# A third layer with three pair buffers, and VectorE's order there by pairs of tiles

## What is computed

```
h = relu(layernorm(x)); x = x + L0(h, adj)    # attention with adj as mask, both signs, elu
h = relu(layernorm(x)); x = x + L1(h, adj)    # relu((D^-1/2 adj D^-1/2 h) W + b)
h = relu(layernorm(x)); x = x + L2(h, adj)    # relu(adj (step(h) sign(W)^T))
h = relu(layernorm(x)); x = x + L3(h, adj)    # (1 - t) h W + t adj (h W)
```

## Time and profile before

| | |
|---|---|
| median of 3 runs | 964.89 us (964.3 to 965.39) |
| the profiled execution | 965.67 us, span of its records 964.0 us |
| PE busy | 933.9 us, 97% of the span |
| DVE, ACT, POOL busy | 743.3, 540.9 and 94.1 us |
| third layer | about 698 to 779 us from the span's start |
| fourth layer | about 779 to 964 us |

### The profile page before, as it was taken

The page is one execution under the profiler, slowest core; times in us unless marked ns, Lnnn a source line. Parts: engine busy times, 40 slices in busy tenths (PEclk is TensorE's granted clock), DMA queues, the critical chain, the costliest instruction groups (busy, mean ns, idle before and its releaser), DMA issues.

```text
span 964.0 us, 18964 instructions
## 1 busy us (share of the span) xinstructions
PE 933.9 (97%) x7105; PEld 689.2 (71%) x7105; DVE 743.3 (77%) x1112; ACT 540.9 (56%) x934; POOL 94.1 (10%) x206
## 2 busy tenths in 40 slices
PE   9889999999999999999999999999999989999995
PEld 8457788888888888888888455555788845555553
DVE  7697899999999999999996776656447755655664
ACT  6476899999999999999985611111223331111010
POOL 4100001000010001000030000000024430000000
PEclk9899999999999999999999999999999999999998
DMA  4915276677576666658312425655247726666642
GB/s 178 96 45 77 23 100 76 66 89 96 48 96 83 81 66 86 86 51 109 46 39 100 173 94 203 211 183 203 114 181 281 276 79 213 215 227 205 201 153 65
DMA packets 39883, 120.80 MB, mean 125 GB/s; under 512 B 4604, under 2 KB 24597, under 8 KB 39701
## 3 DMA queue, kind: packets, MB, share of 16 engines
q1 hardware_dynamic: 27653, 97.94, 29.0%
q0 software_dynamic: 10944, 21.30, 25.5%
q10 hardware_dynamic: 1232, 0.85, 0.3%
HBM read 169.48 MB, written 14.50 MB: 191 GB/s over the span
## 4 chain that ended last, share of the span: by engine, by line
PE 84%; DVE 7%; ACT 3%; issue 2%; POOL 2%; DMA 0%; POOLq 0%; DVEq 0%; ACTq 0%
PE f_ya L1318 23%; PE f_yb L1318 23%; PE f_ya L1495 14%; PE f_ya L1433 12%; DVE f_gb L1856 2%; PE f_ya L1269 2%; PE f_yb L1404 2%; PE f_yb L1376 2%; PE f_yb L1269 1%; PE f_ya L1442 1%; POOL f_gv L960 1%; ACT f_ubuf L1184 1%; ACT f_x_mat L1186 1%; DVE f_stats L1600 1%; PE f_yb L1302 1%
## 5 line engine op out<-in xcount | busy, mean ns | idle before, releaser
L1318 PE MATMUL f_ya<-f_x_mat,f_s_mat 128*128 128x257 f16 x2028 | 334.6, 273 | 1.9 <-DVE f_x_mat L1664 1.9
L1318 PE MATMUL f_yb<-f_x_mat,f_s_mat 128*128 128x257 f16 x2028 | 333.2, 273 | 0.0
L1318 PEld LDWEIGHTS f_yb<-f_x_mat,f_s_mat 128*128 128x128 f16 x2028 | 198.2, 98 | 24.8
L1318 PEld LDWEIGHTS f_ya<-f_x_mat,f_s_mat 128*128 128x128 f16 x2028 | 194.5, 98 | 27.2 <-issue 2.8
L1030 ACT ACTIVATE f_gb<-f_e_tile,f_expc 128x256 f32<-128x256 f32 x338 | 144.5, 494 | 9.3 <-DVE f_s_mat L1694 9.3
L1856 DVE SCALAR_TENSOR_TENSOR f_gb<-f_gb 128x1664 f32<-128x1664 f32 x52 | 97.7, 1886 | 18.0 <-DMA f_gb<-adj_dram 18.0
L1689 DVE SCALAR_TENSOR_TENSOR f_s_mat<-f_wm,f_s_mat 128x1792 f16<-128x1792 f32 (+1 forms) x52 | 98.4, 1892 | 12.1 <-ACT f_s_mat L1041 8.5
L1683 DVE TENSOR_TENSOR f_wm<-f_gb,f_a 128x1792 f32<-128x1792 f32 (+1 forms) x52 | 98.1, 1887 | 3.2 <-issue 1.6
L1684 DVE SCALAR_TENSOR_TENSOR f_gb<-f_gb,f_a 128x1792 f32<-128x1792 f32 (+1 forms) x52 | 98.1, 1887 | 0.0
L1694 DVE SCALAR_TENSOR_TENSOR f_s_mat<-f_gb,f_s_mat 128x1792 f16<-128x1792 f32 (+1 forms) x52 | 98.0, 1886 | 0.0
L1041 ACT ACTIVATE f_s_mat<-f_wm 128x1792 f16<-128x1792 f32 (+1 forms) x52 | 82.5, 1587 | 22.0 <-DVE f_wm L1683 20.9
(11 more groups left out here) (185 smaller groups left out, 938.2 us busy)
## 6 DMA issues: line engine op xcount, KB each, us to landing
f_gb<-adj_dram SPq DMA_DIRECT2D x52, 832.0 KB, 5.0
f_a<-f_a_dram SPq DMA_DIRECT2D x23, 832.0 KB, 5.9
f_wm<-f_a_dram SPq DMA_DIRECT2D x16, 832.0 KB, 4.6
f_rows<-adj_dram POOLq DMA_DIRECT2D x24, 416.0 KB, 8.2
f_a<-adj_t_dram POOLq DMA_DIRECT2D x26, 224.0 KB, 4.9
f_a_dram<-f_a SPq DMA_DIRECT2D x26, 224.0 KB, 5.3
f_a<-adj_t_dram POOLq DMA_DIRECT2D x26, 192.0 KB, 6.9
f_a_dram<-f_a SPq DMA_DIRECT2D x26, 192.0 KB, 4.2
```

Of the source, the lines that this page charges most:

```text
L1318: return pe.matmul(bank[:, 0:F + 1], s_mat[:, j, side, i], x_mat[:, j, x_side, 0:F + 1], start=start, stop=stop)
```

## The change

Two things change, both in the third layer.

The first is the buffers and loads. Pairs 3 to 12 go through a ring of three buffers (`wide[0][:, 0]`, `a8[:, 0]`, `a8[:, 1]`) in place of two, and after pair q is done, pair q + 3 is loaded, where it was pair q + 2. Slot 0 of the fourth layer is loaded after pair 2 (before: after pair 2 too), slots 3, 2 and 1 after pairs 10, 11 and 12 (before: slot 1 after pair 3, slots 2 and 3 after pairs 11 and 12). PE's hardware loop over pairs 5 to 12 becomes straight code.

The second is VectorE's order. A pair is now `update(2q)`, `update(2q + 1)`, then the check for pairs 1 to 10, then `norm(2q)`, `norm(2q + 1)`.

```diff
+        def ring2():
+            return [(wide[0][:, 0], extra_here[0], 3), (a8[:, 0], pair_here[2, 0], 1), (a8[:, 1], pair_here[2, 1], 2)]
...
                     if q == 1:
                         load_pair(2, 4, 0)
                         load_pair(2, 5, 1)
-                    elif q < 4:
-                        load_slot(q - 2)
-                    elif q < PAIRS - 2:
-                        load_pair(2, q + 2, q % 2)
+                    elif q == 2:
+                        load_slot(0)
+                    elif q < PAIRS - 3 and q % 3 == 0:
+                        load_extra(q + 3, 0)
+                    elif q < PAIRS - 3:
+                        load_pair(2, q + 3, q % 3 - 1)
                     else:
-                        load_slot(q - PAIRS + 4)
+                        load_slot(PAIRS - q)
...
                 pair2(2, 0, 16, wide[0][:, 1], extra_here[1])
-                pair2(3, 1, 16, wide[0][:, 0], extra_here[0])
-                pair2(4, 0, 32, a8[:, 0], pair_here[2, 0])
-                with pe.Fori(0, (PAIRS - 5) // 2) as k:
-                    for i in range(2):
-                        pair2(2 * k + 5 + i, 1 - i, 16 * k + 32 + 16 * i, a8[:, 1 - i], pair_here[2, 1 - i])
+                for q in range(3, PAIRS):
+                    rows, here, loads = ring2()[q % 3]
+                    pair2(q, q % 2, 16 * ((q - loads) // 3 + 1), rows, here)
...
                             if layer == 2:
                                 update(t, p, k, r=r)
-                                if not (first and p == 0):
-                                    norm(t - 1, 1 - p)
+                                if p == 1 and 0 < k <= CHECKS1 + 4 - CHECKS2:
+                                    check(CHECKS2 + k - 1, (CHECKS2 + k - 1) % 2)
+                                if p == 1:
+                                    norm(t - 1, 0)
+                                    norm(t, 1)
                                 continue
...
                         for q in range(1, PAIRS):
                             pair(q, False, r=q % 2)
-                            if CHECKS2 + q - 1 < CHECKS1 + 4:
-                                check(CHECKS2 + q - 1, (CHECKS2 + q - 1) % 2)
...
-                    if layer == 2:
-                        norm(TILES - 1, 1)
```

## The result

The changed kernel takes 981.24 us (median of 5 runs, 981.03 to 981.36). The kernel before, run beside it, took 964.3 us (5 runs, 961.8 to 965.39). The ratio of the runs is 1.0185 with a 95% interval of 1.0167 to 1.0202 (that of the two medians is 1.0176): **1.9% slower**. The profiled execution took 981.03 us with a span of 979.2 us. In the new file the same statements stand a few lines lower: L963 of before is L969, L956 is L962, L960 is L966, the check L1856 is L1860, the update L1893 is L1897, the low half L1916 is L1920, and PE's L1483 and L1495 are L1489 and L1499.

A forecast was written before the change was run, and what follows sets the result against it. PE was taken as the bound, except in the third layer's loop through VectorE, GpSimd and ScalarE. 710.73 + 6.23 + 10 x 7.62 + 6.23 + 4.15 = 803.54 against 787.20, so 964.89 + 16.3 = 981.2 us; range 972 to 988.5.

The forecast's parts named there:

- the sum: VectorE's new third-layer order: two pairs of 6.23 us and ten of 7.62 move tile 24's low half by +16.3 us.
- The loads, nothing: Third-layer loads through three buffers, and the fourth layer's slots: off the chain, hidden, worth nothing either way.
- A pair without a check, 6.23 us: Third layer, pairs 0 and 11: next update waits behind both tiles' GpSimd and ScalarE rounds, 6.23 us a pair.
- A pair with a check, 7.62 us: Third layer, pairs 1 to 10: check delays GpSimd's L963, VectorE waits 1.2 us per low half, period 7.62 us.
- The cause, the check holding GpSimd up: Third layer: the check's two SBUF inputs hold GpSimd's L963 until 0.09 us after the check, at U+4.43.
- Low half of tile 24 at 803.54 us: End of the third layer: tile 24's low half moves from 787.20 to 803.54 us, +16.3 us.
- The clock at no cost: PE's granted clock: third-layer idling of 1.9 us in 7.6 costs nothing; border gap grows to about 4.3 us.
- up to 1.6 us: Border of third and fourth layers: possible clock cost if the slow stretch after PE's gap doubles.
- PE's gaps put down to L1893: Changed profile, third layer: PE gaps of about 1.9 us attributed to the update L1893, none to a load.
- The other half of the rule: GpSimd's power, begun before the check, holds the check off: some 0.15 us a pair, 982.7 us in all; not used.
- Rival 3: Third layer: VectorE no longer waits, PE bounds at 5.67 us a pair; -5.0 us, 959.9 us; chance 0.04.
- Rival 2: Third layer: check holds GpSimd's power (L960) as well, period 8.33 us; +23.4 us, 988.3 us; chance 0.05.

The follow-up runs named there:

- run 1: Changed kernel's new buffers, loads and straight PE loop, but VectorE's order of before: 964.9 us against 964.88 for the kernel before, ratio 0.9998.
- run 2: Kernel before with only VectorE's new order, keeping its two buffers and loads: 981.73 us, ratio 1.0184 to the kernel before.
- run 3: Changed kernel without the third layer's ten checks, a one-column memset signalling in place of each: 966.95 us, ratio 1.003 to the kernel before.
- run 4: Changed kernel with the third layer's ten checks reading their second input from PSUM instead of SBUF: 964.92 us, ratio 1.0009 to the kernel before.
- run 5: Changed kernel with each of the ten checks cut into two instructions of 832 columns: 979.7 us, ratio 1.0162 to the kernel before.
- run 6: Kernel before plus the three-buffer ring, each low half two tiles after its update, small tensors four deep: 954.22 us, ratio 0.9896.
- run 7: Kernel before with its two buffers and loads, each low half two tiles after its update, small tensors four deep: 954.44 us, ratio 0.9895.
- run 8: Changed kernel with its order by pairs, but the low halves are those of the pair before, small tensors four deep: 954.13 us, ratio 0.9893.

## Why the prediction was right

The mechanism was the one that the sum used, and runs 1 to 8 bear it out step by step. That 981.2 us met 981.24 so closely is luck: the sum was added to a median of three runs, and the runs of before beside the changed kernel lie between 961.8 and 965.39 us.

- **The loads, nothing:** right, shown by runs 1 and 2. No gap of PE is put down to a load any more, VectorE's period stayed at 6.32 us, and the stretch is 77.1 us against 77.0.
- **A pair without a check, 6.23 us:** 716.73 - 710.49 = 6.24 us between the first two updates. Without checks, a pair in the middle takes 6.15 (run 3).
- **A pair with a check, 7.62 us:** 7.65. L963's counterpart ends 0.07 us after the check (0.09 predicted), the two waits of VectorE are 1.18 and 1.20 us (1.2 each). The 0.03 us that are missing come from the check's start, 0.15 us after the last statistics instead of the 0.10 I took from an update, less the 0.02 by which L969 ends sooner.
- **The cause, the check holding GpSimd up:** run 4 shows it by taking away one SBUF input and nothing else on VectorE's timeline. That without the checks about 6.2 us a pair are left, set by two rounds in a row, is shown by run 3 (6.15 us), and that what exceeds PE's 5.68 us is a wait in VectorE's queue by runs 6 to 8.
- **Low half of tile 24 at 803.54 us:** 803.45. The third layer began 0.24 us earlier, so the shift inside it is 16.5 us against 16.3. The medians differ by 16.9 us; the forecast of 981.2 us stood against a median of 964.89, and the five runs beside the changed kernel had 964.3.
- **The clock at no cost:** right in this trace. It stayed at 1.00 beside gaps of 1.8 us in the third layer, and fell at the border as before: the 41 matmuls behind it took 10.71 us in both. That part varies from execution to execution: behind the same gap of 4.08 us they took 11.95 us in run 2 and 10.37 in run 4, so the "up to 1.6 us" of the prediction was a fair allowance.
- **PE's gaps put down to L1893:** not in the changed profile, which gives them no name. Their size, 1.8 us, and their ends just behind an update are as predicted, and run 2 has the name.
- **The other half of the rule**, that a power under way keeps VectorE out for its whole length (in the Trainium skill, "SBUF — State Buffer", the words on the whole instruction for two SBUF inputs stand in the section "SBUF: two separate sides"), would have given 982.7 us. The trace of before speaks against it: three more VectorE instructions with two SBUF inputs begin inside the 9.27 us power of the earlier trace rows, at 497.74, 499.81 and 501.79, and take 2.10, 2.03 and 2.02 us, where their lines take 2.02 on average. The power of 726.35 to 726.92 overlaps the check's start at 726.87, and in run 4 the check, beside which no GpSimd operation was held, starts after the last statistics as late as here (730.76 to 730.91). An overlap of 0.05 us can't tell much; what no run tested is a check issued in the middle of a one-column power.
- **A place where the sum was right though its step was not:** in pair 1, L969 came 0.09 us ahead of the check and got through in 0.21 us. Then the second tile's first operation was held instead, 1.74 us (719.79), to the same end, and the next update still came 724.38 - 716.73 = 7.65 us after the last. Either victim gives the same period, because the second tile's round can't start before the check ends.

Rival 3, VectorE without waits and PE as the bound, is what runs 6 to 8 made of the kernel. Its price of 959.9 us was too high by 6 us: I had counted only the pairs, and left out PE's idle time at the border, 0.43 + 0.68 + 2.51 = 3.6 us in the trace of before, and the slow clock behind it (41 matmuls in 10.71 us; at the pace of run 6, 65 in 14.19, they take 8.95), which go as well.

Rival 2 (the power held as well) didn't occur in the changed kernel, but its mechanism exists: with the lag of two tiles, a power that started 0.06 us after a check (736.20) took 2.24 us instead of 0.57:

```profile
736.26 2.24 POOL L966 TENSOR_TENSOR f_gv<-f_gv,f_minus_half 128x1 f32<-128x1 f32 x1
```

## What to carry to other kernels

An engine that works in order pays for every round through other engines that begins and ends within one turn of its loop. Count these rounds in the new order before counting work: here VectorE had about 5 us of work a pair and a period of 7.65. Let the result of a round be picked up one turn later, which costs only deeper small buffers, before buying deeper large ones. And before a long VectorE instruction with two SBUF inputs is moved beside GpSimd's small operations, look whether anyone waits for these: one of them can be held until the VectorE instruction ends.

## What the runs showed of the hardware

- A hold-up by the shared interface has no entry among the waits. It shows as one GpSimd record that is too long (1.72 us for one column) and ends 0.07 to 0.09 us after the VectorE record, and as an unnamed "issue" piece of 1.55 us in the chain.
- Some 0.1 us decide who is held. An operation that starts 0.05 or 0.09 us ahead of the VectorE instruction gets through (732.67 in run 4, 719.47 after the change); one that starts 0.06 us behind it is held to its end (736.26 in run 6). So a kernel with less work can be slower: 6.15 us a pair without checks, 5.99 with checks that read one SBUF tensor.
- Cutting the VectorE instruction in two doesn't halve the damage when several small operations follow each other: 7.55 against 7.65 us a pair.
- With gaps of 1.8 us before each 5.8 us of matmuls, PE's granted clock stayed at its upper level, 1.00 from 711 to 795 us.
